# One-core ViT layer: v in fp32r for two images at a time, scores in 32x32 pieces, first-half probabilities in rows of 32

## The chip, the cores and the metric

The kernel runs on one core of one Trainium2 chip. The metric is device time in microseconds (us) of that core; the median of three runs is given. Engines are called PE (TensorE, with PEld for its weight loads), DVE (VectorE), ACT (ScalarE) and POOL (GpSimd). SBUF is the on-chip working memory, PSUM the memory that PE writes, in eight banks of 128 x 512 fp32.

## The reference

64 images give 49 patches each, with a class token 50 tokens of 256 values. Patches are RMS-normalised, quantised, and multiplied by a quantised weight. Then comes causal attention at three "scales", whose windows all reach beyond the 50 tokens, so that each is a plain causal attention over 50 tokens with weights of its own; each is followed by a projection and a layer norm, and the three are mixed by a last projection. A quantised gated feed-forward network ends the layer.

```
h   = embed(quantised patches)                               # (64, 50, 256)
x   = layer_norm(h)
for i in range(3):                                           # three scales
    q, k, v = x @ Wq[i].T, x @ Wk[i].T, x @ Wv[i].T          # 16 heads of 16
    s   = 4 * q k^T, masked above the diagonal
    e   = exp(s - max(s));  w = e / (sum(e) + 1e-6)
    o_i = layer_norm((w v) @ Wo[i].T)
h   = h + layer_norm(concat(o_i) @ Wout.T);  y = layer_norm(h);  out = h + ffn(y)
# feed-forward: fake-quantised silu(y Wg) * (y Wu), whose largest absolute value over
# everything sets the step of the quantisation before the down projection
```

## The kernel before

**Stages.** The first block does embedding and attention for eight groups of eight images (`GROUPS`, `GB`), and quantises the weights of the feed-forward network in between. The second block (from line 1484 on POOL, 1507 on DVE, 1598 on PE) does gate and up projections for all groups, finds the largest product, then does the down projection.

**Units.** A group has six *s* steps: three scales times two sets of four images (`QB = 4`). Each s step has two *units* u, e = 0 and e = 1: queries 0 to 24 against keys 0 to 24 (`WIDTH[0] = 25`), and queries 25 to 49 against all 50 keys (`WIDTH[1] = 50`). So the kernel has 48 s steps and 96 units. Four images' queries stand in PSUM rows 0, 32, 64 and 96.

**Steps of one s step.** On PE `k` and `q` (line 1265) are six fp32r matmuls of 400 columns each for every half of a scale's 256 rows: a value is cut into a high and a low fp32r part, and three products are added. `v` (lines 1281, 1285) is done in plain fp32, image by image: even heads into rows 0 to 49, odd heads into rows 64 to 113. POOL `spread` (line 875) multiplies k by a mask over head rows into `k_bd`, with four copies for each 64 rows, in two instructions per pair of images. PE `scores` (line 1299 for the mask, 1308 for the products) works in tiles of 64 rows by 32 columns, 16 products a unit; e picks one half of `ps_s`, so two units' scores can stand in PSUM at once, and the step waits for `scores_read` of the unit before the last. DVE `max` (1085) finds the maxima, `soft` (1089) subtracts them and so frees `ps_s`; ACT takes the exponential (780); DVE sums and inverts (1097, 1102); POOL multiplies (884). PE `turn_p` (1323) transposes the probabilities, eight transpositions into two banks for each unit, since a head has a row of 64 also where 25 keys are used; ACT copies them to `pT` (789), two copies a unit. PE `heads` (1334) multiplies by v, which ACT copied block-diagonally to `v_bd` in two copies (773). PE `project` (1350) follows.

**Order.** Each engine walks its own list, written out by hand in `AT` (tick numbers per kind of step, sorted by `engine_order`). Steps of several groups interleave. All PE results but the scores go round four PSUM banks (`ps_w`, `bank_plan`); a step waits until the bank's reader, four fills back, is through. Engines issue in order: a waiting instruction holds up all behind it.

## Time and profile before

| what | value |
|---|---|
| median of three runs | 819.95 us (814.86 to 820.36) |
| the profiled execution | 819.57 us, of which 817.7 us are the span from the first to the last instruction |
| mean granted TensorE clock | 0.959 of full speed |
| PE busy | 728.1 us, 89% of the span |
| DVE busy | 649.7 us, 79% |
| POOL busy | 544.5 us, 67% |
| ACT busy | 519.0 us, 63% |

Rough stages of the span: 0 to 56 us loading, embedding of the first images and preparation of weights; 56 to about 697 us attention; about 712 to 778 us gate and up projections; the rest is the down projection and the store. A busy share is an average over its stretch. An engine that is hardly ever idle sets the pace of a stage; what the others do costs time only where they make that one wait.

### The profile page before, as it was taken

The page shows a single profiled execution, that of the slowest core. Times are in us where ns is not written, and L with a number is a line of the kernel's source. Part 1 is how long each engine was busy: PE and PEld are TensorE (multiplying, and loading weights), DVE is VectorE, ACT ScalarE, POOL GpSimd, SP SyncE. Part 2 cuts the span into 40 slices and gives each one's busy share as a digit, 9 for nine tenths or more (in the row PEclk, how much of TensorE's full clock was granted, in tenths as well). Part 3 has the DMA queues.
Part 4 walks back from the last instruction along what each step waited for, and adds up shares of the span by engine and source line. Part 5 has one row for each costly group of instructions (what it writes and reads, how often), then busy time and mean ns, then how long its engine had stood idle before and what let it go on. Part 6 is the DMA issues. An engine that isn't in the chain of part 4 may idle for free. (4 is left out here: it accounts for less than half of the span.)

```text
span 817.7 us, 28887 instructions
## 1 busy us (share of the span) xinstructions
PE 728.1 (89%) x11302; PEld 573.7 (70%) x11302; DVE 649.7 (79%) x1346; ACT 519.0 (63%) x1085; POOL 544.5 (67%) x817
## 2 busy tenths in 40 slices
PE   1488999999999999999999999999999999377565
PEld 1265887788878787878777887878888787244354
DVE  4679676889788888888898789888987895758857
ACT  3546857646766576667556675675666665278684
POOL 2569757685786688858857866887768764421165
PEclk9869999999999999999999999999999999679979
DMA  8200000000000000000000000000101000000014
GB/s 243 88 15 31 14 20 17 18 17 18 18 17 17 18 16 18 18 18 31 3 18 18 16 18 18 18 31 3 38 3 38 20 3 20 0 1 0 0 32 129
DMA packets 14968, 22.09 MB, mean 27 GB/s; under 512 B 1972, under 2 KB 11446, under 8 KB 14840
## 3 DMA queue, kind: packets, MB, share of 16 engines
q1 hardware_dynamic: 14404, 19.91, 7.7%
q8 instruction: 90, 1.47, 0.7%
q10 hardware_dynamic: 436, 0.40, 0.2%
q14 instruction: 38, 0.31, 0.1%
HBM read 17.03 MB, written 3.28 MB: 25 GB/s over the span
## 5 line engine op out<-in xcount | busy, mean ns | idle before, releaser
L875 POOL TENSOR_TENSOR k_bd<-kT,rmask 128x400 f32<-128x400 f32 x192 | 167.4, 901 | 19.2 <-ACT kT L757 11.8
L884 POOL TENSOR_TENSOR prob<-prob,rsum 128x400 f32<-128x400 f32 x96 | 117.2, 1235 | 25.3 <-DVE rsum L1102 25.3
L789 ACT COPY pT<-ps_w 128x400 f32<-128x400 f32 x192 | 85.4, 507 | 29.1 <-PE ps_w L1323 28.3
L1285 PE MATMUL ps_w<-wv_sb,xf 128*50 128x128 f32 x1536 | 99.2, 272 | 0.0
L1323 PE MATMUL ps_w<-pack,prob 128*128 128x128 f32 x768 | 95.1, 275 | 1.8 <-DVE hidden L1062 0.9
L1350 PE MATMUL ps_w<-oy_hi,o_hi 128*128 128x512 f32 x192 | 93.6, 488 | 0.0
L1323 PEld LDWEIGHTS ps_w<-pack,prob 128*128 128x128 f32 x768 | 84.1, 141 | 11.9 <-issue 8.5
L1085 DVE TENSOR_REDUCE nmax<-ps_s 128x16 f32<-128x400 f32 x96 | 72.5, 770 | 9.7 <-PE ps_s L1308 9.2
L1097 DVE TENSOR_REDUCE rsum<-prob 128x16 f32<-128x416 f32 x96 | 74.1, 781 | 6.4 <-ACT prob L780 6.3
L803 ACT ACTIVATE ps_w<-ps_w 128x256 f32<-128x256 f32 x96 | 35.5, 370 | 68.8 <-PE ps_w L1350 68.4
L1285 PEld LDWEIGHTS ps_w<-wv_sb,xf 128*50 128x50 f32 x1536 | 78.1, 125 | 0.3
L780 ACT ACTIVATE prob<-prob 128x400 f32<-128x400 f32 x96 | 67.2, 714 | 15.9 <-DVE prob L1089 15.5
L1350 PE MATMUL ps_w<-oy_lo,o_hi 128*128 128x512 f32 x192 | 76.1, 396 | 0.0
L773 ACT COPY v_bd<-ps_w 50x512 f32<-50x512 f32 x96 | 55.8, 581 | 31.8 <-PE ps_w L1285 30.0
L1089 DVE TENSOR_TENSOR prob<-ps_s,nmax 128x400 f32<-128x400 f32 x96 | 72.7, 769 | 3.5 <-ACT pT L789 3.1
L1350 PE MATMUL ps_w<-oy_hi,o_lo 128*128 128x512 f32 x192 | 75.5, 393 | 0.0
L1308 PE MATMUL ps_s<-k_bd,qT 64*25 64x200 f32 (+1 forms) x3072 | 71.2, 293 | 0.0
L1265 PE MATMUL ps_w<-xh,qk_hi 128*128 128x400 f32 x192 | 70.2, 366 | 1.1 <-POOL xl L864 0.9
L1265 PE MATMUL ps_w<-xl,qk_hi 128*128 128x400 f32 x192 | 66.5, 346 | 0.0
L1265 PE MATMUL ps_w<-xh,qk_lo 128*128 128x400 f32 x192 | 66.4, 346 | 0.0
L889 POOL TENSOR_TENSOR ln<-ln,ln_eps 128x1 f32<-128x1 f32 x96 | 19.3, 201 | 69.0 <-ACT ps_w L803 68.6
L891 POOL TENSOR_TENSOR ln<-ln,neg_half 128x1 f32<-128x1 f32 x96 | 53.4, 557 | 7.5
(216 smaller groups left out, 1756.0 us busy)
## 6 DMA issues: line engine op xcount, KB each, us to landing
x_in<-in_x SPq DMA_DIRECT2D x64, 147.0 KB
out<-hidden SPq DMA_DIRECT2D x16, 200.0 KB
pT<-in_tok_w SPq DMA_DIRECT2D x1, 768.0 KB, 6.6
hidden<-in_wq SPq DMA_DIRECT2D x1, 768.0 KB, 8.4
k_bd<-in_wk SPq DMA_DIRECT2D x1, 768.0 KB, 9.2
wv_sb<-in_wv SPq DMA_DIRECT2D x1, 768.0 KB, 8.9
hidden<-in_wout SPq DMA_DIRECT2D x1, 768.0 KB, 8.9
hidden<-in_wo SPq DMA_DIRECT2D x1, 768.0 KB, 11.0
```

Source lines behind the costliest of these rows:

```text
L780: nc.scalar.activation(pr, pr, ACT.Exp).then_inc(exp_ready, 1)
L789: nc.scalar.copy(pT[:, s % 2, 4 * a:4 * a + 4, :, e * LQ:(e + 1) * LQ], ps_w[:, bank].rearrange("p (j t) -> p j t", j=4)[:, :, 0:QB * LQ]. ...
L875: last = nc.gpsimd.tensor_tensor(k_bd[:, v % KBD, c], kT[:, w % 2, c, 2 * p * L:(2 * p + 2) * L].unsqueeze(1).broadcast_to([P, HR, 2 * L]) ...
L884: nc.gpsimd.tensor_tensor(pr, pr, rsum[:, s % 2, e, 1].unsqueeze(2).broadcast_to([P, H, WIDTH[e]]), ALU.mult).then_inc(prob_ready, 1)
L1085: nc.vector.tensor_reduce(top, s_ps, AX.X, ALU.max, negate=True).then_inc(max_ready, 1)
L1089: nc.vector.tensor_tensor(prob[:, s % 2, e, :, 0:WIDTH[e]].rearrange("p (r h) t -> p r h t", r=2), s_ps, top.unsqueeze(3).broadcast_to([P, ...
L1097: nc.vector.tensor_reduce(rsum[:, s % 2, e, 0], prob[:, s % 2, e, :, 0:WIDTH[e] + 1], AX.X, ALU.add).then_inc(sum_ready, 1)
L1265: mm = nc.tensor.matmul(G[:, 0:GT], wt[:, w, q, k, c * P:(c + 1) * P], xt[:, k], start=(t == 0), stop=(t == 3 * KC - 1))
L1285: mm = nc.tensor.matmul(G[row:row + L, cols], xf[:, k, tokens], wv_sb[:, w, k, e], start=False, stop=(k == KC - 1), skip_group_check=True)
L1308: mm = nc.tensor.matmul(ps_s[32 * b:32 * b + LQ, e, r, c * HR * W:(c + 1) * HR * W], qT[rows, w % 2, c, first:first + LQ], k_bd[rows, v % ...
L1323: mm = nc.tensor.transpose(G[:, j * P:(j + 1) * P], flat[:, (4 * a + j) * P:(4 * a + j + 1) * P], pack[:])
L1350: mm = nc.tensor.matmul(G[:], ot[:, s % 2, c, 2 * (p % 2):2 * (p % 2) + 2].rearrange("p b t -> p (b t)"), wt[:, w, c], start=False, stop=( ...
```

## The change

- `v`: weights are cut into fp32r parts `wv_hi` and `wv_lo` (one ACT cast, one DVE subtraction), and two images are one stationary operand of 128 columns (`xh` and `xl` now give each image 64 columns). A step is two times one bias matmul and six fp32r matmuls of 256 columns. ACT takes v apart with four copies of 50 x 256 where it had two of 50 x 512.
- `spread`: two copies of k for each 32 rows, one instruction of 128 x 400 per pair of images where it had two.
- `scores`: tiles of 32 rows by 32 columns, 32 products a unit, each of half the columns. The four row groups write four banks, that is all of `ps_s`, for either e. So the step waits for `scores_read` of the last unit: one unit's scores at a time.
- `turn_p`, e = 0: probabilities have rows of 32 (`prob_lo`), so four transpositions into one bank do; ACT takes them apart with four copies of 25 partitions x 400. e = 1 is as before.
- Feed-forward: the maximum over a group's 2400 columns (line 1558) is taken in three pieces of 800, each placed after the next product.
- At the start: four small loads of the mask from ACT's queue, zeroing of `pT`, `v_bd` loaded with Wv first and zeroed once it is cut.
- All lists of `AT` are new. In the new PE list some other work stands between any two steps of scores; in the old one 39 of the 95 neighbours follow each other directly.

```diff
-    order = [... for a in range(2 if step[0] == "turn_p" else 1)]
+    order = [... for a in range(2 if step[0] == "turn_p" and step[1] % 2 else 1)]
...
@@ ACT
+                if kind == "wv_hi":
+                    act.wait_ge(loads["wv"], 16)
+                    nc.scalar.copy(wv_hi[:], by_row(st_v)).then_inc(split_v, 1)
...
                     for row, e in HALVES:
-                        nc.scalar.copy(v_bd[row:row + L, s % 2, :, :, e * HD:(e + 1) * HD],
-                                       ps_w[row:row + L, bank, :].rearrange("p (b j d) -> p b j d", b=QB, j=HP)).then_inc((v_even, v_odd)[e], 1)
+                        for src, b in HALVES:
+                            last = nc.scalar.copy(v_bd[row:row + L, s % 2, b::2, :, e * HD:(e + 1) * HD], v_ps[src:src + L, :, e])
+                    last.then_inc(v_ready, 1)
...
+                    if e == 0:
+                        bank, fill = bank_of(step)
+                        act.wait_ge(filled[bank], fill)
+                        act.wait_ge(zeroed, 4)
+                        for c in range(KC):
+                            for h in (0, 1):
+                                row = 32 * (2 * c + h)
+                                last = nc.scalar.copy(pT[ROWB * h:ROWB * h + LQ, s % 2, c::2, :, 0:LQ],
+                                                      ps_w[row:row + LQ, bank].rearrange(...)[:, :, 0:QB * LQ].rearrange(...))
+                        last.then_inc(pt_read, 1)
...
@@ POOL
                     if j == 0:
+                        pool.wait_ge(v_split, 1)
                         nc.gpsimd.memset(v_bd[:], 0.0).then_inc(zeroed, 1)
...
-                    for c in range(KC):
-                        last = nc.gpsimd.tensor_tensor(
-                            k_bd[:, v % KBD, c], kT[:, w % 2, c, 2 * p * L:(2 * p + 2) * L].unsqueeze(1).broadcast_to([P, HR, 2 * L]),
-                            rmask[:].unsqueeze(2).broadcast_to([P, HR, 2 * L]), ALU.mult)
-                    last.then_inc(kbd_ready, 1)
+                    nc.gpsimd.tensor_tensor(
+                        k_bd[:, v % KBD], kT[:, w % 2, :, 2 * p * L:(2 * p + 2) * L].unsqueeze(2).broadcast_to([P, KC, 2, 2 * L]),
+                        rmask[:].unsqueeze(1).unsqueeze(3).broadcast_to([P, KC, 2, 2 * L]), ALU.mult).then_inc(kbd_ready, 1)
...
@@ PE
-                    for b in range(QB):
-                        cols = slice(b * P, (b + 1) * P)
-                        tokens = slice((QB * q + b) * L, (QB * q + b + 1) * L)
-                        for row, e in HALVES:
-                            nc.tensor.matmul(G[row:row + L, cols], ones16[:, 0:L], bias3[:, (e * NS + w) * P:][:, 0:P],
-                                             start=True, stop=False, skip_group_check=True)
+                    for a in (0, 1):
+                        cols = G[:, a * D:(a + 1) * D]
+                        two = slice(QB * q + 2 * a, QB * q + 2 * a + 2)
+                        nc.tensor.matmul(cols, ones16[:], v_bias[:, w], start=True, stop=False)
                         for k in range(KC):
-                            for row, e in HALVES:
-                                mm = nc.tensor.matmul(G[row:row + L, cols], xf[:, k, tokens], wv_sb[:, w, k, e],
-                                                      start=False, stop=(k == KC - 1), skip_group_check=True)
+                            for xt, wt in ((xh, wv_hi), (xh, wv_lo), (xl, wv_hi)):
+                                mm = nc.tensor.matmul(cols, xt[:, k, two].rearrange("p b t -> p (b t)"), wt[:, w, k], start=False,
+                                                      stop=(k == KC - 1 and xt is xl))
...
-                    pe.wait_ge(scores_read, U * m + u - 1 + AHEAD)
+                    pe.wait_ge(scores_read, U * m + u + AHEAD)
...
                     for c in range(KC):
-                        for r in (0, 1):
-                            rows = slice(r * ROWB, (r + 1) * ROWB)
-                            for b in range(QB):
-                                first = (QB * q + b) * L + e * LQ
-                                v = 2 * s + b // 2
-                                mm = nc.tensor.matmul(ps_s[32 * b:32 * b + LQ, e, r, c * HR * W:(c + 1) * HR * W],
+                        for b in range(QB):
+                            first = (QB * q + b) * L + e * LQ
+                            v = 2 * s + b // 2
+                            for r in range(4):
+                                rows = slice(32 * r, 32 * r + 32)
+                                mm = nc.tensor.matmul(row_ps[32 * b:32 * b + LQ, r, c * 2 * W:(c + 1) * 2 * W],
                                                       qT[rows, w % 2, c, first:first + LQ],
                                                       k_bd[rows, v % KBD, c, :, (b % 2) * L:(b % 2) * L + W],
                                                       start=False, stop=True, skip_group_check=True)
...
-                    for a in (0, 1):
+                    for a in range(1 + e):
                         G = ps_w[:, bank_of(step, a)[0]]
...
@@ DVE, feed-forward
+            def largest(g, j, done):
+                dve.wait_ge(acts_ready, done + T)
+                nc.vector.tensor_reduce(hmx[:, bass.ds(g * FC + 2 * j, 2)], acts[:, 2 * j:2 * j + 2, bass.ds(g * GT, GT)], AX.X, ALU.max,
+                                        apply_absolute_value=True).then_inc(acts_max, 1)
...
+                    if j > 0:
+                        largest(g, j - 1, n)
+                largest(g, FP - 1, g * FP + FP)
```

## Rows read from the trace of the kernel before

**Rows 1.** The page's first part: busy us, share of the span, instructions.
```profile
PE 728.1 (89%) x11302; PEld 573.7 (70%) x11302; DVE 649.7 (79%) x1346; ACT 519.0 (63%) x1085; POOL 544.5 (67%) x817
```

**Rows 2.** Busy time by stretch: stretch, its length, busy us per engine, clock, DMA.
```profile
60.00:80.00 20.00, 15.92 (x300) 12.33 (x299) 19.55 (x22) 12.49 (x20) 19.38 (x17) 0.96 0.10 32
140.00:540.00 400.00, 396.14 (x6713) 321.50 (x6712) 337.51 (x752) 261.28 (x577) 300.61 (x482) 1.00 0.06 18
740.00:760.00 20.00, 14.20 (x96) 7.88 (x96) 17.94 (x17) 17.37 (x31) 3.13 (x3) 1.00 0.00 0
```

**Rows 3.** Waits of PE, 140 to 540 us, the longest: us, times, longest.
```profile
PE ps_s L1299 <- DVE prob L1089: 1.4, 2, 1.2
```

**Rows 4.** Waits of DVE, 140 to 540 us: first and last of 16.
```profile
DVE nmax L1085 <- PE ps_s L1308: 8.2, 9, 3.0
...
DVE acc L1132 <- DVE ln L1130: 0.2, 1, 0.2
```

**Rows 5.** Timeline of PE, 400 to 430 us: start, duration, merged instructions.
```profile
400.49 0.39 PE L1350 MATMUL ps_w<-oy_hi,o_hi 128*128 128x512 f32 x1
400.72 0.40 PE L1350 MATMUL ps_w<-oy_lo,o_hi 128*128 128x512 f32 x1
...
401.28 0.26 PE L1299 MATMUL ps_s<-mask,pick 64*128 64x200 bf16 x2
401.47 0.57 PE L1308 MATMUL ps_s<-k_bd,qT 64*25 64x100 f32 x32
401.97 0.34 PE L1299 MATMUL ps_s<-mask,pick 64*128 64x400 bf16 x2
402.24 0.90 PE L1308 MATMUL ps_s<-k_bd,qT 64*25 64x200 f32 x32
403.08 0.83 PE L1247 MATMUL ps_w<-tokT,x_qT 128*128 128x256 bf16 x6
...
409.35 0.24 PE L1281 MATMUL ps_w<-bias,ones 96*50 96x128 bf16 x2
...
411.36 0.22 PE L1281 MATMUL ps_w<-bias,ones 96*50 96x128 bf16 x2
...
415.44 1.97 PE L1323 MATMUL ps_w<-pack,prob 128*128 128x128 f32 x16
417.25 0.50 PE L1238 MATMUL ps_w<-id,x_q 128*128 128x128 bf16 x6
...
419.81 1.83 PE L1334 MATMUL ps_w<-pT,v_bd 128*32 128x50 f32 x128
421.57 0.24 PE L1281 MATMUL ps_w<-bias,ones 96*50 96x128 bf16 x2
```

**Rows 6.** Groups of instructions by form: busy us, mean ns, idle before.
```profile
L875 POOL TENSOR_TENSOR k_bd<-kT,rmask 128x400 f32<-128x400 f32 x192 | 167.4, 901 | 19.2 <-ACT kT L757 11.8 <-PE ps_s L1308 7.2
L789 ACT COPY pT<-ps_w 128x400 f32<-128x400 f32 x192 | 85.4, 507 | 29.1 <-PE ps_w L1323 28.3
L773 ACT COPY v_bd<-ps_w 50x512 f32<-50x512 f32 x96 | 55.8, 581 | 31.8 <-PE ps_w L1285 30.0
L1085 DVE TENSOR_REDUCE nmax<-ps_s 128x16 f32<-128x800 f32 x48 | 47.0, 980 | 2.4 <-PE ps_s L1308 2.1
L1089 DVE TENSOR_TENSOR prob<-ps_s,nmax 128x800 f32<-128x800 f32 x48 | 46.8, 975 | 0.5 <-ACT pT L789 0.3
L1265 PEld LDWEIGHTS ps_w<-xl,qk_hi 128*128 128x128 f32 x192 | 36.5, 190 | 0.6
L1247 PE MATMUL ps_w<-tokT,x_qT 128*128 128x256 bf16 x192 | 29.0, 292 | 2.5 <-ACT x_qT L737 2.0 <-issue 0.4
L1558 DVE TENSOR_REDUCE hmx<-acts x6 | 15.9, 2653 | 0.9
```

**Rows 7.** PE's timeline cut to 401.465 to 401.472, and to 401.40 to 401.53.
```profile
401.47 0.26 PE L1308 MATMUL ps_s<-k_bd,qT 64*25 64x100 f32 x1
...
401.47 0.31 PE L1308 MATMUL ps_s<-k_bd,qT 64*25 64x100 f32 x8
```

356 lines of the change are left out of this document (193 added, 163 removed), and 131 rows, old and new, of the table AT.

## The prediction

> **What bounds the kernel now.** I read four views, from coarse to fine. The page's first part [rows 1] shows PE busiest, but as a mean over unlike stages. The table by stretch [rows 2] says where: over 400 us in the middle of attention PE is busy 396, DVE 338, POOL 301 and ACT 261, at full clock. The list of PE's waits there [rows 3] has hardly anything: its longest entry is 1.4 us in all. So in attention the time is the sum of PE's steps, and a microsecond taken out of them is a microsecond of the kernel as long as nobody else becomes late. Who would? DVE's waits in the same stretch are 16 entries, first and last in [rows 4], which add up to 47 us. So 400 - 47 = 353 us are taken, by work of 338 and small gaps of 15: DVE is at 88%, nearer to PE than its busy share says. The stretch from 60 to 80 us is another case: POOL and DVE are full and PE is idle for 4 of 20 us. In gate and up projections (740 to 760) DVE is full with 17.9 of 20.
>
> From PE's timeline [rows 5] I take each step from its start to the start of the next. v takes 411.36 - 409.35 = 2.01 us. Scores take 0.69 for e = 0 (401.28 to 401.97) and 1.11 for e = 1 (to 403.08), of which the mask is 0.19 and 0.27. Two transposing steps take 1.81, or 0.91 each. Two steps of heads, 128 matmuls, take 1.76.
>
> **v.** The nearest fp32r matmul, line 1350, has 512 columns and comes every 400.72 - 400.49 = 0.23 us [rows 5], 0.45 ns a column; for 256 columns 0.115. The bias matmul of 256 bf16 columns is like line 1247, six in 0.83 where one lasts 0.29 [rows 5, 6]: (0.83 - 0.29) / 5 = 0.11 from start to start. A half is 0.11 + 6 x 0.115 = 0.80, a step 1.60, and I add 0.05 for the first load: 1.65. Gain 0.36 x 48 = 17 us. The other bound is a load that can't hide behind so short a matmul: the load row of line 1265 says 190 ns [rows 6], which makes 2 x (0.11 + 6 x 0.19) = 2.5 us and a loss of 24. I take the first: the fp32 transpositions load 128 columns as well and come every 0.11 us [rows 5], so a load's record is longer than what it holds up.
>
> **Transpositions, e = 0.** Four for eight: 0.45 of 0.91, times 48, is 22 us. Nothing is unknown here.
>
> **Scores.** 32 products a unit, two matmul instructions each: 64 for 32. Their columns are halved and the tiles doubled, so each tile has half the work, for twice the instructions in all, and what counts is how fast they start. The cut of the timeline [rows 7] shows one lasting 0.26 and eight together 0.31, so eight start within 0.05 us, some 7 ns apart. At the other end are the heads, 1.76 / 128 = 13.8 ns [rows 5], where four tiles share the work, so that the array itself may be what limits. After the last start today's e = 0 takes 0.50 - (0.57 - 0.25) = 0.18 until the next step (with 0.25 for the last matmul). I take 7 ns, the burst's: 0.19 + 0.45 + 0.18 = 0.82 for either e. The pair is 1.64 for 1.80, gain 0.16 x 48 = 8 us. At 13.8 ns it is 2.5, a loss of 34.
>
> The Trainium skill speaks against this part. "TensorE: Matmul & The Clock Gate", section "Back-to-back issue gap", gives about 25 ns as the least distance of two matmuls however few the columns. By it a unit would take 64 x 0.025 + 0.37 = 1.97 us and the change would lose 103 us here. The trace doesn't agree for products in different tiles: 32 of them begin within 0.32 us.
>
> Sum on PE: 17 + 22 + 8 = 47 us of some 640 us of attention. k, q, heads and projections keep their matmuls and columns; the padded rows of `xh` change a stride only.
>
> **The other engines.** POOL: 96 instructions of 0.9 us fall away (line 875, [rows 6]), 86 us in all, and nothing is added but some zeroing at the start; in the stretch it goes from 301 of 400 us to about 247 of 370, or 67%. This helps the ramp at 60 to 80 us. It may help DVE too. The Trainium skill, "SBUF — State Buffer", section "Who interferes with whom", says that VectorE and GpSimd lock one pair of ports against each other; by it DVE gains a few microseconds here, which no row here prices and the sum leaves out.
>
> ACT: for e = 0 four copies of 400 columns for two, at 0.51, are 1.0 us more for each of 48 steps [rows 6]: 49 us. v: four of 256 columns; from 400 columns at 0.507 and 512 at 0.581 a column is 0.66 ns, so 0.41 each, 1.65 for 1.16, or 24 us. Together 73 us over attention: from 65% of 641, 419 us, to 492 of 594, or 83%. It has no price while its copies come in time; they free PE's banks, four fills back.
>
> DVE: same work in attention, in a stage that is 7% shorter: 353 of 370, 95%. This is the cover that gets thin.
>
> **The new wait.** One unit's scores at a time: the step of unit u + 1 waits for `soft` of u, and behind it on PE stands everything else, since PE issues in order; ACT, POOL and DVE then wait for PE. After a unit's scores DVE needs 0.98 for the maxima and 0.975 for the subtraction (e = 1; [rows 6]), with hand-overs about 2.2 us; e = 0 about 1.3. I added up the new PE list with the times above: of 95 distances between scores, 9 hold less than 2 us of other PE work and 22 less than 2.5. A DVE that is a little late (it has other steps between) makes PE wait there. I put this, with DVE and ACT nearly full, at 0.15 us a unit: 14 us. Net in attention 47 - 14 = 33.
>
> **Feed-forward.** A group's maximum in three pieces: 800 columns are 2.65 / 3 = 0.88 at least and 0.98 by line 1085 [rows 6], so 0 to 0.3 us more on the full engine in each of eight groups; against it a piece fills the gap before a group's last product, and the last group's end has two pieces behind the last product for one of 2.65. I take 1 us gain, plus or minus 2.
>
> **Start.** wv is cut (ACT about 1.5 us, DVE about 2.3), `v_bd` is zeroed only then, and POOL's next steps stand behind that wait; against it are the faster spreads. I take 0, plus or minus 4.
>
> Working against the profiled execution, 819.6 us (817.7 of span), whose difference to the median of 819.95 is nothing: 819.6 - 33 - 1 = 786 us.
>
> **The rivals.**
> - *All of it arrives.* The order fits, nobody is late, and the ramp gives 4: 819.6 - 47 - 1 - 4 = 768. For it: PE's waits are near nothing now. Against: DVE at 95%. Chance 0.15.
> - *Half is eaten.* DVE or ACT is late more often and PE waits 0.35 us a unit, 34 us: 819.6 - 47 + 34 - 1 = 806. For it: the two shares. Chance 0.18.
> - *A bound of a matmul is wrong.* Loads of 190 ns make v a loss: 786 + 41 = 827; or products start at the heads' pace: 786 + 42 = 828. Against: the transpositions, the burst. Chance 0.10 for both.
> - *Slower by the single buffer.* Place: the mask matmul at the head of scores. PE waits for `soft` unit by unit; it decides at 47 / 96 = 0.5 us a unit, and with 0.75 it is 819.6 - 47 + 72 = 845. Against: other work is placed between all scores, where 39 of 95 were neighbours. Chance 0.08.
> **How the numbers follow.** The forecast, 786 with 776 to 799 of its own, has 0.48. For faster by over 1% (below 811; about what a measurement here can tell) I add 0.48, 0.15 and most of the half-eaten case: 0.78. Within 1% get the rest of it and most of the wrong bounds: 0.12. Slower: 0.10. The range of 8 in 10 goes from the full gain to just past the half-eaten case, 765 to 815; beyond lie the slow cases with their 0.2.
>
> **What would show it.** v from start to next start: 1.6 to 1.7 (2.5: loads don't hide). Scores: about 0.8 for either e, 64 starts 7 ns apart (14: the other bound). Transpositions of e = 0: 0.45. PE's waits at the mask line for DVE `prob`: some 14 us in attention; 50 or more and the single buffer has won. DVE's waits shrink from 47 of 400 to some 20 of 370. POOL's spread is 96 x 0.9. If ACT stands at 83% and PE waits at `turn_p` or `heads` for ACT's `pT`, the four copies are the reason. I am wrong if PE's steps shrink by 47 us and the time doesn't follow, or if they don't shrink.

## The result and the profile after

The changed kernel takes 806.48 us (median of 4 runs, 804.51 to 808.14) where the kernel before, beside it, takes 819.55 (814.86 to 820.36): ratio 0.9851, with a 95% interval of 0.9808 to 0.9895. The profiled execution took 806.6 us with a span of 804.8, against a span of 817.7 before. That is 13 us faster, where 34 were forecast; 806 is the number of the rival in which half of the gain is eaten; whether its mechanism is the one that acted is taken up at the end.

First the page of the changed kernel and its table by stretch, with the columns of [rows 1] and [rows 2]:

```profile
PE 710.1 (88%) x13126; PEld 567.1 (70%) x13126; DVE 639.9 (80%) x1363; ACT 584.2 (73%) x1278; POOL 462.3 (57%) x728
```

```profile
60.00:80.00 20.00, 17.95 (x353) 13.75 (x351) 16.25 (x27) 15.38 (x25) 15.16 (x19) 1.00 0.11 33
140.00:540.00 400.00, 386.00 (x7931) 318.17 (x7931) 338.59 (x760) 301.19 (x694) 248.25 (x416) 1.00 0.06 19
740.00:760.00 20.00, 17.24 (x112) 9.18 (x110) 20.00 (x25) 17.50 (x31) 3.24 (x3) 1.00 0.00 0
```

In the 400 us in the middle of attention PE has lost 10 us of its fullness, ACT has gained 40, POOL has lost 52 and DVE stands where it was, since the stage did not get shorter. That is the second reading. I cut both traces at the start of the first k or q product, of the last product of attention's projections and of the last maximum of the feed-forward part:

| part, us | before | after | difference |
|---|---|---|---|
| up to the first k or q product | 55.8 | 52.3 | -3.5 |
| attention, to its last projection | 643.1 | 643.9 | +0.8 |
| from there to the last maximum (gate and up) | 76.3 | 68.1 | -8.2 |
| the rest | 42.6 | 40.5 | -2.1 |

So the stage at which the change was aimed gave nothing, and the 13 us come from around it (the rest holds the last maximum itself, which is a piece of 0.9 us where it was 2.6). Within attention I add up PE's time by step (each matmul from its start to the next one's start, idle time apart):

| PE in attention, us | before | after | forecast difference | measured |
|---|---|---|---|---|
| v | 99.7 | 82.7 | -17 | -17.0 |
| transposed probabilities | 87.7 | 71.0 | -22 | -16.7 |
| scores | 87.7 | 95.8 | -8 | +8.1 |
| k and q | 112.0 | 118.8 | 0 | +6.8 |
| projections | 158.0 | 159.4 | 0 | +1.4 |
| all other steps | 87.0 | 92.3 | 0 | +5.3 |
| PE idle | 10.8 | 23.7 | +14 | +12.9 |

Of the 5.3 in "other steps", 3.4 are two short steps (`bo_fold`, `y_spread`) that stood before the first k product and now stand behind it; that is the 3.5 us of the start, so the start gained nothing by itself.

A part of the growth is the granted clock, which the prediction took as full. In the changed kernel 15.4 us of attention lie at half clock: the first 5.1, which are the end of a stretch that began before attention, and three stretches of 3.4, each begun 0.4 to 2 us after PE had stood still for 1.9, 1.4 and 1.4 us. In the kernel before it is one stretch of 6.8 us. The three stretches, with the columns of [rows 2], and k and q products in the second one:

```profile
453.40:456.80 3.40, 3.40 (x79) 2.92 (x79) 0.68 (x1) 2.82 (x6) 2.79 (x3) 0.50 0.34 100
600.10:603.50 3.40, 3.39 (x11) 2.99 (x12) 3.02 (x5) 2.71 (x7) 1.62 (x3) 0.51 0.03 5
692.30:695.70 3.40, 3.40 (x9) 2.36 (x8) 2.99 (x11) 0.48 (x2) 1.92 (x5) 0.50 0.01 2
```

```profile
601.91 0.54 PE L1307 MATMUL ps_w<-xh,qk_lo 128*128 128x400 f32 x1
602.24 0.54 PE L1307 MATMUL ps_w<-xh,qk_hi 128*128 128x400 f32 x1
```

These products come every 0.33 us where they come every 0.19 at full clock. By such distances my estimate is that half clock makes up 2 of the 6.8 us of k and q, 1.8 us of the transpositions and all of the 1.4 of the projections, some 5 us of PE's steps in all.

The timeline of PE after, with start, duration and merged instructions, as in [rows 5]:

```profile
403.90 0.22 PE L1340 MATMUL ps_s<-mask,pick 32*128 32x100 bf16 x4
404.05 0.80 PE L1349 MATMUL ps_s<-k_bd,qT 32*25 32x50 f32 x64
404.78 0.45 PE L1307 MATMUL ps_w<-xh,qk_hi 128*128 128x400 f32 x1
405.07 0.35 PE L1307 MATMUL ps_w<-xl,qk_hi 128*128 128x400 f32 x1
...
405.82 0.35 PE L1307 MATMUL ps_w<-xh,qk_lo 128*128 128x400 f32 x1
406.02 0.28 PE L1323 MATMUL ps_w<-bias,ones 96*128 96x256 bf16 x1
...
406.26 0.28 PE L1326 MATMUL ps_w<-wv_lo,xh 128*128 128x256 f32 x1
406.38 0.28 PE L1326 MATMUL ps_w<-wv_hi,xl 128*128 128x256 f32 x1
...
407.70 1.03 PE L1364 MATMUL ps_w<-pack,prob_hi 128*128 128x128 f32 x8
...
409.32 0.27 PE L1340 MATMUL ps_s<-mask,pick 32*128 32x200 bf16 x4
409.52 0.96 PE L1349 MATMUL ps_s<-k_bd,qT 32*25 32x100 f32 x64
410.41 0.51 PE L1280 MATMUL ps_w<-id,x_q 128*128 128x128 bf16 x6
...
418.65 0.66 PE L1364 MATMUL ps_w<-pack,prob_lo 128*128 128x128 f32 x4
419.14 0.27 PE L1323 MATMUL ps_w<-bias,ones 96*128 96x256 bf16 x1
```

v takes 407.70 - 406.02 = 1.68 us and its matmuls come every 0.12; the four transpositions take 419.14 - 418.65 = 0.49; the scores take 0.88 (403.90 to 404.78) and 1.09 (409.32 to 410.41), together 1.97 for 1.80 before. The k and q matmuls come every (405.82 - 405.07) / 4 = 0.187 us.

PE's waits and DVE's in the same 400 us, with the columns of [rows 3] and [rows 4], the longest of each:

```profile
PE ps_w L1297 <- ACT v_bd L793: 2.1, 2, 1.1
PE ps_s L1340 <- DVE prob_lo L1131: 2.0, 3, 1.3
PE ps_w L1280 <- issue: 1.9, 1, 1.9
PE ps_w L1385 <- DVE o_lo L1151: 1.5, 1, 1.5
```

```profile
DVE nmax L1127 <- PE ps_s L1349: 11.8, 13, 3.9
DVE acc L1162 <- issue: 7.7, 11, 2.8
```

There are 13 kinds of waits of PE, 13.0 us in all, where there were 6 with 3.7 us. None is over 2.1 us: they are small ones, for ACT and for DVE, all over the stage. No single one has taken the place of the work removed. DVE's waits add up to 45 us where they were 47; the prediction's sign was some 20 of 370. The costliest groups of ACT and POOL, with the columns of [rows 6]:

```profile
L813 ACT COPY pT<-ps_w 25x400 f32<-25x400 f32 x192 | 94.7, 493 | 7.7 <-PE ps_w L1364 5.1
L793 ACT COPY v_bd<-ps_w 50x256 f32<-50x256 f32 x192 | 70.5, 367 | 18.8 <-PE ps_w L1326 16.3
```

```profile
L915 POOL TENSOR_TENSOR k_bd<-kT,rmask 128x400 f32<-128x400 f32 x96 | 83.5, 885 | 36.6 <-ACT kT L775 21.9 <-PE ps_s L1349 14.7
```

Over attention the durations of ACT's instructions, added up, went from 474 to 539 us (+65), POOL's from 495 to 414 (-81), DVE's from 585 to 581. Neighbours overlap a little, so the busy times are smaller: ACT 420 to 489, POOL 477 to 403, DVE 531 to 529.

### The profile page after: what moved, and what is told of

Read it like the earlier page. It is cut to its first block and busy times, and to the rows that moved or that the text cites. A ratio compares the mean times of both kernels' runs of the same rounds, so it can differ in the third digit from the quotient of the medians.

```text
span 804.8 us, 32634 instructions
## 1 busy us (share of the span) xinstructions
PE 710.1 (88%) x13126; PEld 567.1 (70%) x13126; DVE 639.9 (80%) x1363; ACT 584.2 (73%) x1278; POOL 462.3 (57%) x728
## 5 line engine op out<-in xcount | busy, mean ns | idle before, releaser
L915 POOL TENSOR_TENSOR k_bd<-kT,rmask 128x400 f32<-128x400 f32 x96 | 83.5, 885 | 36.6 <-ACT kT L775 21.9
L813 ACT COPY pT<-ps_w 25x400 f32<-25x400 f32 x192 | 94.7, 493 | 7.7 <-PE ps_w L1364 5.1
L923 POOL TENSOR_TENSOR prob_hi<-prob_hi,rsum 128x800 f32<-128x800 f32 x48 | 75.1, 1565 | 37.0 <-DVE rsum L1144 37.0
L1127 DVE TENSOR_REDUCE nmax<-ps_s 128x16 f32<-128x400 f32 x96 | 74.1, 772 | 23.8 <-PE ps_s L1349 23.1
L1349 PE MATMUL ps_s<-k_bd,qT 32*25 32x50 f32 (+1 forms) x6144 | 84.9, 231 | 0.4 <-issue 0.4
L793 ACT COPY v_bd<-ps_w 50x256 f32<-50x256 f32 x192 | 70.5, 367 | 18.8 <-PE ps_w L1326 16.3
L1349 PEld LDWEIGHTS ps_s<-k_bd,qT 32*25 32x25 f32 x6144 | 61.6, 97 | 13.2 <-issue 0.7
L1326 PE MATMUL ps_w<-wv_hi,xh 128*128 128x256 f32 x192 | 62.1, 323 | 0.0
L923 POOL TENSOR_TENSOR prob_lo<-prob_lo,rsum 128x400 f32<-128x400 f32 x48 | 42.6, 888 | 28.6 <-DVE rsum L1144 28.5
L1326 PE MATMUL ps_w<-wv_lo,xh 128*128 128x256 f32 x192 | 54.1, 282 | 0.0
L1326 PE MATMUL ps_w<-wv_hi,xl 128*128 128x256 f32 x192 | 54.0, 281 | 0.0
L1364 PE MATMUL ps_w<-pack,prob_hi 128*128 128x128 f32 x384 | 52.3, 279 | 0.5 <-ACT v_bd L793 0.3
```

Source lines behind the costliest of these rows:

```text
L793: last = nc.scalar.copy(v_bd[row:row + L, s % 2, b::2, :, e * HD:(e + 1) * HD], v_ps[src:src + L, :, e])
L813: last = nc.scalar.copy(pT[ROWB * h:ROWB * h + LQ, s % 2, c::2, :, 0:LQ], ps_w[row:row + LQ, bank].rearrange("p (j t) -> p j t", j=4)[:, : ...
L915: nc.gpsimd.tensor_tensor(k_bd[:, v % KBD], kT[:, w % 2, :, 2 * p * L:(2 * p + 2) * L].unsqueeze(2).broadcast_to([P, KC, 2, 2 * L]), rmask ...
L923: nc.gpsimd.tensor_tensor(pr, pr, rsum[:, s % 2, e, 1].unsqueeze(2).broadcast_to([P, H, WIDTH[e]]), ALU.mult).then_inc(prob_ready, 1)
L1127: nc.vector.tensor_reduce(top, s_ps, AX.X, ALU.max, negate=True).then_inc(max_ready, 1)
L1326: mm = nc.tensor.matmul(cols, xt[:, k, two].rearrange("p b t -> p (b t)"), wt[:, w, k], start=False, stop=(k == KC - 1 and xt is xl))
```

## The experiments

Differences "by the ratio" are against the kernel before or the changed kernel, as 819 us times the difference of the ratios; the interval of a ratio is 2 to 6 thousandths to either side, so 2 to 5 us. A difference between two runs has both intervals in it: against the changed kernel, whose own is 4 thousandths, it is good to 4 to 6 us. Where an edit's diff is shown cut, "..." stands for what is left out. Attention's length and PE's steps are those of one profiled execution, and how long it stood at half clock differs too (in us of attention: before 6.8, changed 15.4).

### The feed-forward part by itself

The kernel before, with only the maximum in three pieces:

```diff
-                nc.vector.tensor_reduce(hmx[:, bass.ds(g * FC, FC)], acts[:, :, cols], AX.X, ALU.max, ...
...
+                    if j > 0:
+                        largest(g, j - 1, n)
+                largest(g, FP - 1, g * FP + FP)
```

> The kernel before, with only the maximum of the feed-forward network taken in three pieces. Theory 1 (read from the two traces): the gain of the whole change sits behind attention, where the period of a group of gate and up fell from 6.45 to 5.69 us; this piece alone gives it, 819.6 - 10 = about 810 us, and a period of 5.7. Rival (the prediction's own step): the pieces give 1 us, plus or minus 2, and the period falls because of something else, so about 819 and a period of 6.3 to 6.5.

Measured: 813.1 us, ratio 0.9915 (0.988 to 0.9949), so 7 us. Attention 644.1; to the last maximum 71.5 (-4.8), the rest 40.5 (-2.1). DVE's timeline in gate and up projections, first before, then with this edit:

```profile
743.53 2.65 DVE L1558 TENSOR_REDUCE hmx<-acts  x1
746.10 0.98 DVE L1553 TENSOR_TENSOR acts<-ps_s,gate 128x800 f32 x1
...
748.85 0.99 DVE L1553 TENSOR_TENSOR acts<-ps_s,gate 128x800 f32 x1 [0.55 <-ACT gate L1449]
749.98 2.65 DVE L1558 TENSOR_REDUCE hmx<-acts  x1
```

```profile
741.83 0.98 DVE L1558 TENSOR_TENSOR acts<-ps_s,gate 128x800 f32 x1
742.73 1.86 DVE L1548 TENSOR_REDUCE hmx<-acts  x2
744.52 0.98 DVE L1558 TENSOR_TENSOR acts<-ps_s,gate 128x800 f32 x1
...
746.63 0.97 DVE L1548 TENSOR_REDUCE hmx<-acts  x1
747.53 0.98 DVE L1558 TENSOR_TENSOR acts<-ps_s,gate 128x800 f32 x1
```

A group goes from 749.98 - 743.53 = 6.45 us to 747.53 - 741.83 = 5.70. The pieces hardly lengthen the work (three times 0.9 from start to start for 746.10 - 743.53 = 2.57), and they fill the gaps in which DVE stood between products: together 0.75 us a group, and two pieces less behind the last product. So 7 of the 13 us are this edit. The prediction's own 1 us, the rival here, is out. Another 3.4 come from the handover, which only the changed kernel has (last projection to last maximum: 68.1 against 71.5). The traces put them on DVE: its last instruction of attention ends 8.8 us after the last projection starts (705.0 - 696.2), with this edit alone 12.2 us (712.1 - 699.9). The new order leaves it less to do at the end; which entry of the list does it was not tried.

### ScalarE: two of the four copies left out

```diff
-                        for c in range(KC):
+                        for c in range(1):
                             for h in (0, 1):
                                 ... last = nc.scalar.copy(pT[ROWB * h:..., s % 2, c::2, :, 0:LQ], ...)
```

> The changed kernel, with two of the four copies of the first-half probabilities left out (the half of the heads keeps zeros there, so the output is another): 96 instructions and 47 us less on ACT. Theory 2 (ACT at 75 to 80% of attention holds PE's banks too long): 8 us or more faster, 798 or less. Theories 1 and 3: within 2 us of 806.5.

Measured: 795.97 us, ratio 0.9715 (0.9671 to 0.9759), 11 us less than the changed kernel. Attention 632.4, 11.5 less, of which PE's idle time is 5.7 (23.7 to 18.0) and 5.8 lie inside the steps. Of these some 4 are the clock: 6.6 us of attention are at half clock, where it was 15.4. ACT's work has a price although ACT is busy for only 75% of the stretch.

### Padded rows in the kernel before

`xh` and `xl` with rows of 64 for images of 50 tokens, as the change has them, in the kernel before. To have the space, the low part of the output weights is replaced by the high part.

```diff
-    xh = sb(att, "xh", [P, KC, GT], F32R)
+    xh = sb(att, "xh", [P, KC, GB, ROWB], F32R)
...
-  nc.tensor.matmul(G[:, 0:GT], wt[:, w, q, k, c * P:(c + 1) * P], xt[:, k], ...
+  nc.tensor.matmul(G[:, 0:GT], wt[:, w, q, k, c * P:(c + 1) * P], xt[:, k, :, 0:L], ...
```

> The kernel before, with the rows of xh and xl padded from 50 to 64 columns for each image; for want of SBUF the low part of the output projection's weights is not kept (that matmul reads the high part again, so the output is less exact; every instruction stays). Theory 1: the padded rows make the 400-column matmuls of k and q slower, 0.19 us from start to start for 0.18, and the kernel 6 to 8 us slower, 826 to 828. Rival: k and q are longer in the changed kernel through hidden waits, and padding costs nothing: 820, plus or minus 1.5, and 0.18 us.

Measured: 818.48 us, ratio 0.9987 (0.9963 to 1.0012). Its timeline, with the x columns read in runs of 50 out of 64:

```profile
404.82 0.35 PE L1265 MATMUL ps_w<-xl,qk_hi 128*128 128x400 f32 x1
...
406.74 0.35 PE L1265 MATMUL ps_w<-xh,qk_lo 128*128 128x400 f32 x1
```

Ten matmuls on, 1.92 us: 0.192 each, against 0.182 in the kernel before. The k and q steps take 115.4 us for 112.0, PE's idle time falls from 10.8 to 7.8, and the time is unchanged. Theory 1 was right on the 0.19 and wrong on the time, its rival the other way round. So "the padded rows of `xh` change a stride only" was wrong for the steps, and no harm to the time could be measured. That is only a weak sign that PE's time doesn't count one for one, since this execution had no half clock in attention where the kernel before has 6.8 us of it. Without that the padding costs k and q some 4.4 us, and with the 2 us of half clock this makes up nearly all of their 6.8.

### The first half in rows of 64 again

The changed kernel, with eight transpositions and two copies for e = 0 as before:

```diff
-    prob_lo = sb(att, "prob_lo", [P, 2, H, 32])
+    prob_lo = sb(att, "prob_lo", [P, 2, H, ROWB])
...
-                    for a in range(1 + e):
+                    for a in (0, 1):
```

> The changed kernel, with the first-half probabilities in rows of 64 again: eight transpositions and two copies a unit. PE has some 20 us more to do and ACT 49 us less. Theory 2 (ACT is the late one): both cancel, 806 plus or minus 6. Theory 3 (only PE's own work counts): 806 + 20 = 826.

Measured: 833.05 us, ratio 1.0183 (1.0132 to 1.0233), 27 us slower than the changed kernel. Attention 668.3 (+24.4): steps +19.3, idle +5.1, although ACT has 46 us less. Here PE's work counted in full, and ACT's relief did not show. The time is 7 us beyond even theory 3's 826. Each of these steps also fills two banks of the ring where the change fills one; whether that is the surplus was not tried.

### Score products of 64 rows again, with two buffers and with one

The changed kernel with the scores in tiles of 64 rows by 32 columns, `k_bd` with four copies again, made by 192 instructions of POOL. To have the space, the low part of the output weights is replaced by the high part in the projections. The two runs differ in one line, the wait of the step:

```diff
-                        nc.gpsimd.tensor_tensor(k_bd[:, v % KBD], ...[P, KC, 2, 2 * L]..., ALU.mult)
+                        for c in range(KC):
+                            last = nc.gpsimd.tensor_tensor(k_bd[:, v % KBD, c], ...[P, HR, 2 * L]..., ALU.mult)
...
-                    pe.wait_ge(scores_read, U * m + u + AHEAD)
+                    pe.wait_ge(scores_read, U * m + u - 1 + AHEAD)    # two buffers only
```

> The changed kernel with its new order, but scores in tiles of 64 rows by 32 columns as before, two buffers, and POOL's spread in two instructions (86 us more on POOL); for want of SBUF the low part of the output projection's weights is replaced by the high part. Scores take 0.17 us less a pair, 8 us in all. Theory 1 (the single buffer costs waits): those 8 and another 8 or more, 790 or less. Rival (the single buffer costs nothing in this order): 806.5 - 8 = 798, plus or minus 3. If POOL's larger load matters: 803 or more.

> The same as the run with 64x32 scores and two buffers, but the step waits for the subtraction of the last unit as in the changed kernel: the pair differs in nothing but the single buffer. Theory 1: 8 us or more slower than its partner. Rival: within 2 us of it.

Measured: with two buffers 818.71 us, ratio 1.0013 (0.9982 to 1.0044), attention 656.4; with one 827.83, ratio 1.0108 (1.0071 to 1.0145), attention 666.5. The stretch from 140 to 540 us with two:

```profile
140.00:540.00 400.00, 373.10 (x5775) 293.67 (x5774) 333.15 (x742) 295.28 (x683) 292.22 (x471) 1.00 0.06 17
```

and one product step of either half in its timeline:

```profile
404.01 0.57 PE L1351 MATMUL ps_s<-k_bd,qT 64*25 64x100 f32 x32
...
408.30 0.90 PE L1351 MATMUL ps_s<-k_bd,qT 64*25 64x200 f32 x32
```

Two things follow. The single buffer costs 8 to 10 us here, so it is a real price, far from that of the rival that ends slower (72). And the 64-row products are the shorter ones on PE (scores 88.5 us for 95.8), yet with them and two buffers the kernel is 12 to 14 us slower, and PE's idle time is 43.2 for 23.7. POOL has 85 us more (292 of 400 for 248), and PE's list of waits in the 400 us now names POOL's products of the probabilities (5.5 us of 26.5), which the changed kernel's doesn't; its two longest entries are for DVE (4.5 and 4.2). So the case of load on POOL, 803 or more, is the one that holds, and both theories on the buffer (790 or less, 798) are out for the run with two. What the small products bring is POOL's relief, not PE's time. The pair prices the single buffer for 64-row products. For the 32-row products, which fill all four banks in one unit, no run has a second buffer.

### v in plain fp32 again

```diff
-    xh = sb(att, "xh", [P, KC, GB, ROWB], F32R)
+    xh = sb(att, "xh", [P, KC, GB, L], F32R)
...
-                            for xt, wt in ((xh, wv_hi), (xh, wv_lo), (xl, wv_hi)):
-                                mm = nc.tensor.matmul(cols, xt[:, k, two]..., wt[:, w, k], ...
+                            for row, e in HALVES:
+                                mm = nc.tensor.matmul(G[row:row + L, cols], xf[:, k, QB * q + b], wv_sb[:, w, k, e], ...
```

> The changed kernel with one part undone: v again in plain fp32 over unpadded `xh` and `xl`, 2 copies of v_bd a unit pair of halves instead of 4; scores, maxima and rows of 32 stay as changed. On TensorE v's step goes back from 1.7 to 2.0 us (+17 us over 48 steps) and the k and q steps lose the 3.4 to 6.8 us that the padded rows cost; ScalarE gets some 24 us back. Theory A (TensorE's own time counts nearly in full, ScalarE's lateness with the slope of the run without two copies, 10.5 us for 47): 806.5 + 17 - 5 - 5 = 813, from 810 to 817. Rival B (what TensorE is given there only becomes a wait, since the vector engines set the time): attention within 2 us of the changed kernel's 643.9, or shorter by ScalarE's 5 us, and the time 801 to 808.

Measured: 817.31 us, ratio 0.9988 (0.9959 to 1.0017), 11 us slower than the changed kernel; attention 651.9 (+8.0), steps +9.9 (v +18.7, k and q -7.1), idle -2.0. Theory A's 810 to 817 is just missed, B's 801 to 808 is out. In the changed kernel's order, work added to PE counts nearly in full, although ACT has 15 us less here.

### Work moved off ScalarE, and taken off it

The first edit moves 32 instructions from ACT to POOL, the second leaves them on ACT and does them on 64 of 768 columns.

```diff
-                    nc.scalar.activation(x_t[:], x_in[:, p % 2], ACT.Identity, scale=xs[:, 6, p:p + 1], bias=magic[:])
+                    nc.gpsimd.tensor_scalar(x_t[:], x_in[:, p % 2], xs[:, 6, p:p + 1], MAGIC, ALU.mult, ALU.add)
```

> The changed kernel with 32 instructions of 1.03 us (the rounding shift of x in the group stages) moved from ScalarE to GpSimd, at the same place of the order; everything is computed. ScalarE is relieved of 33 us, GpSimd, at 62% in the stretch from 140 to 540 us, gets some 33 to 50. Theory A (ScalarE is late): by the slope of 10.5 us for 47, the time falls by 7 us to 799 or 800, with TensorE's idle time in attention falling from 23.7 to about 20. Rival B (GpSimd's load slows VectorE and comes late itself, as in the run with 64-column scores and two buffers): no gain or a loss, 806 to 812, and VectorE's instructions of x_q longer than 697 ns.

```diff
-                    nc.scalar.activation(x_t[:], x_in[:, p % 2], ACT.Identity, ...
+                    nc.scalar.activation(x_t[:, 0:64], x_in[:, p % 2, 0:64], ACT.Identity, ...
```

> The changed kernel with the rounding shift of x in the group stages done on 64 of 768 columns (the output is another): ScalarE has 32 instructions of some 0.3 us for 1.03 us, 23 us less over attention, and no other engine gets or loses work. In the run that moved these instructions to GpSimd nothing was gained; here GpSimd isn't loaded for it. Theory A (ScalarE's load as a whole makes it late): with the slope of the run without two copies (10.5 us for 47 us) the time falls by 5 us, to 801 or 802, TensorE's idle time in attention from 23.7 to some 20. Theory B (what costs is the latency of the four copies between the transpositions and what waits for their bank and for `pT`, not ScalarE's load): less than 2 us, 804 to 807.

Measured: moved, 808.2 us, ratio 0.9896 (0.9863 to 0.9928), attention 643.0 and idle 25.3: no gain, perhaps a loss. Taken off, 801.17 us, ratio 0.9754 (0.9732 to 0.9776), 8 us less than the changed kernel by the ratio and 5 by the median, attention 636.7, idle 20.6. In attention the durations of ACT's instructions add up to 28 us less in the first and 17 less in the second. Of the 7.2 us of attention some 4 lie inside PE's steps and go with the clock (6.6 us at half clock for 15.4). So it is ACT's load as such, not only the copies' place, that costs, and 28 us more on POOL, in a stretch where it was busy for 62%, seem to cost about what 28 us less on ACT give.

### VectorE: half of the sum, half of the maximum

```diff
-  nc.vector.tensor_reduce(rsum[...], prob[e][:, s % 2, :, 0:WIDTH[e] + 1], AX.X, ALU.add)
+  nc.vector.tensor_reduce(rsum[...], prob[e][:, s % 2, :, 0:WIDTH[e] // 2 + 1], AX.X, ALU.add)
```

> The changed kernel with one edit that changes the result: the sum of the probabilities is taken over half of the columns, which takes about 35 us from VectorE in attention and nothing from any other engine. Theory A (VectorE is late, too): the time falls by 8 us or more, to 798 or less. Rival B (VectorE isn't what TensorE waits for; ScalarE and the single buffer of scores are): less than 2 us, 804 to 807.

```diff
-  nc.vector.tensor_reduce(top, s_ps, AX.X, ALU.max, negate=True)
+  nc.vector.tensor_reduce(top, s_ps[:, :, :, 0:WIDTH[e] // 2], AX.X, ALU.max, negate=True)
```

> The changed kernel with the maximum taken over half of the columns of each head's scores (the output is another): VectorE has 37 us less in attention, about as much as the 35 us less of the run with half the sum, which gave 3 us. But this work lies between a unit's last product and the release of the only score buffer, so the buffer is held 0.4 us (first half 0.2, second 0.5) less per unit, 96 times. Theory A (TensorE's waits and steps at the single buffer are what costs): clearly more than 3 us, 8 to 15, so 792 to 799, and TensorE's idle time in attention from 23.7 to 15 or less. Theory B (the buffer isn't what costs in this order; only VectorE's load): 3 us like the half sum, 802 to 805.

Measured: the sum, 803.73 us, ratio 0.9827 (0.9768 to 0.9885), attention 640.9 (-3.0), idle 21.9; the maximum, 801.83 us, ratio 0.9756 (0.9732 to 0.9779), attention 639.3 (-4.6), idle 23.2. Both take 30 us from DVE. The engine that looked fullest after PE gives back least: 2 to 3 us, which is within the noise. The same work between the last product and the release of `ps_s` gives 5 to 8, which is theory A's sign, but the idle time that it named (15 or less) did not come. That the two edits differ is not shown: their intervals meet, and the 1.6 us between their attentions are less than the clock can make, since the run with half the sum has 15.0 us of attention at half clock and the run with half the maximum 7.0. With the pair above, the buffer has a price of some us, and its size in this order stays open.

### Copies split between two engines

Two of the four copies on DVE, with a semaphore of their own:

```diff
-                        for c in range(KC):
+                        for c in (0,):
...
+                if kind == "turn_lo":
+                    for h in (0, 1):
+                        row = 64 + 32 * h
+                        last = nc.vector.tensor_copy(pT[ROWB * h:ROWB * h + LQ, s % 2, 1::2, :, 0:LQ], ps_w[row:row + LQ, bank]...)
```

> The changed kernel, everything computed, with two of the four copies of the first half's transposed probabilities moved from ScalarE to VectorE: ScalarE has 47 us less, VectorE 48 x 2 x 0.5 = 48 us more (from 85% in the stretch from 140 to 540 us to about 96%), and the four copies lie on two engines side by side, 1 us from the transpositions to the last copy for 2. Theory A (latency of the copies): most of the 10.5 us of the run that left two copies out, less what VectorE's load costs by the half-sum run's slope (3 us for 35, so 4): 799 to 801. Theory B (VectorE, nearly full, comes late for the single score buffer): no gain or a loss, 806 to 820, with VectorE's waits in attention gone and TensorE's idle time above 24.

Measured: 849.65 us, ratio 1.0331 (1.0302 to 1.0361). DVE's group of these copies and PE's two longest waits in the 400 us:

```profile
L1147 DVE COPY pT<-ps_w 25x400 f32<-25x400 f32 x96 | 55.1, 574 | 10.4 <-PE ps_w L1381 8.6
```

```profile
PE ps_s L1357 <- DVE prob_lo L1135: 4.8, 5, 2.2
PE ps_w L1324 <- DVE pT L1147: 3.6, 2, 2.1
```

That is beyond both theories. Attention is 692.3 us, 48 longer: 35 of it are PE's idle time (59), 13 lie in PE's steps. 36 us of attention are at half clock, so most of the 13 go with the clock and not with work: PE's pauses seem to be paid for twice. DVE is busy for 583 of the 692 us, 84%, where it was 82% with 54 us less work. So the stage grew by nearly as much as DVE's work, and the 16% in which it stands idle were not room for it. It can be relieved without much gain and not loaded.

### The same questions in the order of the kernel before

The runs so far stand in the changed kernel's order. Three runs in the old order take the two sides of the sum apart: v over one of two parts of its contraction (PE 42 us less), ACT's copies for e = 0 cut into rows 0 to 63 and 64 to 127 (ACT 49 us more), and both.

```diff
-                        for k in range(KC):
-                            for row, e in HALVES:
-                                mm = nc.tensor.matmul(G[row:row + L, cols], xf[:, k, tokens], wv_sb[:, w, k, e], ...
+                        for row, e in HALVES:
+                            mm = nc.tensor.matmul(G[row:row + L, cols], xf[:, 0, tokens], wv_sb[:, w, 0, e], ...
```

> The kernel before with v's product over one of the two 128-row parts of its contraction (the output is another): four of each eight fp32 matmuls fall away, 0.22 us four times a step, 48 steps: 42 us less on TensorE, about what the prediction expected of v and the transpositions together (39), and nothing changes on another engine. Theory A (TensorE's sum sets attention, microsecond for microsecond, as the prediction read the waits): 819.5 - 42 = 777, from 775 to 781. Theory B (ScalarE, VectorE and GpSimd are so near that a part becomes waits): 25 us or less, so 794 or more, with TensorE's idle time in attention growing from 10.8 to 25 or more.

```diff
-                        nc.scalar.copy(pT[:, s % 2, ...], ps_w[:, bank]...).then_inc(pt_read, 1)
+                        for rows in (slice(0, 64), slice(64, P)) if e == 0 else (slice(0, P),):
+                            last = nc.scalar.copy(pT[rows, s % 2, ...], ps_w[rows, bank]...)
+                        last.then_inc(pt_read, 1)
```

> The kernel before with ScalarE's two copies of the first half's transposed probabilities each cut into two of 64 rows: four copies of 0.5 us for two, 96 x 0.5 = 49 us more on ScalarE in attention, the same data, TensorE, VectorE and GpSimd unchanged. Theory A (ScalarE's load and the latency of these copies are paid in part, 0.24 us per us as in the changed kernel): 10 to 15 us slower, 829 to 835. Theory B (the prediction's reading: no price while the copies come in time, since ScalarE goes from 65% to 73% only): less than 2 us, 818 to 822.

> Both edits at once in the order of the kernel before: TensorE 42 us less, ScalarE 49 us more (the output is another). Theory A (the added copies are what eats the gain): the time lies 15 us or more above the run with TensorE's work alone, since the stage is shorter and ScalarE fuller: 792 to 802 if that one is at 777. Theory B (they don't): within 4 us of that run. Theory C (the parts add up): the sum of the two single effects within 3 us.

Measured:

| | us | ratio to before | attention | PE's steps | PE idle |
|---|---|---|---|---|---|
| before | | 1 | 643.1 | 632.1 | 10.8 |
| PE 42 less | 806.2 | 0.9807 (0.9758 to 0.9857) | 628.8 | 597.2 | 31.3 |
| ACT 49 more | 844.93 | 1.0288 (1.0228 to 1.0348) | 665.3 | 642.1 | 23.1 |
| both | 828.19 | 1.0086 (1.0052 to 1.012) | 643.0 | 603.3 | 39.5 |

The stretch from 140 to 540 us of the three, in this order:

```profile
140.00:540.00 400.00, 383.64 (x6430) 302.90 (x6414) 345.22 (x770) 266.05 (x588) 306.69 (x490) 1.00 0.06 18
```

```profile
140.00:540.00 400.00, 389.83 (x6590) 311.43 (x6589) 327.96 (x731) 284.50 (x613) 289.16 (x462) 1.00 0.06 18
```

```profile
140.00:540.00 400.00, 377.10 (x6165) 294.84 (x6167) 337.00 (x750) 289.90 (x632) 298.07 (x478) 1.00 0.06 17
```

and PE's longest waits in the first:

```profile
PE ps_w L1322 <- DVE acc L1120: 3.6, 6, 1.9
PE ps_s L1298 <- DVE prob L1089: 3.0, 1, 3.0
PE ps_w L1284 <- issue: 1.7, 2, 0.9
```

Theory B holds in the first: v's steps lost 40.2 us, attention 14.3, and 20.5 came back as idle time, with no engine but PE over 87%. Taking a microsecond from PE was worth 0.35 to 0.4. The second is beyond even theory A: 49 us on an engine busy for 65% cost 22 to 24 us, nearly half of each. PE's list of waits has six entries for ACT's `pT` (L790), none over 1.2 us; the kernel before has none for it. 10 of the 22 us are not in its idle time but inside its steps, though PE's work is the same and only 3.4 us are at half clock: 7.4 of them in the transpositions, whose banks these copies free. A transposition's record lasts 0.28 us where the starts are 0.11 apart, so a short wait of the next one doesn't show as idle time. By the ratios the two effects add up (-16 and +24 make +8, measured +7, theory C). The attention lengths (+7.9 by addition, -0.1 measured) don't contradict it: the profiled execution of both edits took 821.45 us, 6.7 less than the median of its ten. So removing 42 us of PE and adding 49 of ACT is no gain but a loss of some 7 us. The changed kernel's own trade is of this kind, -34 us in v and the transpositions for +65 of ACT; it has POOL's relief on top.

## Why the prediction was right and wrong

**What bounds the kernel.** This step failed first: "in attention the time is the sum of PE's steps, and a microsecond taken out of them is a microsecond of the kernel as long as nobody else becomes late". The sum was right as bookkeeping (632.1 of 643.1) and wrong as a slope. That PE hardly waits [rows 3] shows that every release comes just in time, not that it comes early. With 42 us less on PE, the releases of DVE, POOL and ACT were late by half of that (idle time +20.5). The condition, "as long as nobody else becomes late", was read from shares (88, 75 and 65% in the stretch), and a share says nothing of the distance between a release and the step that needs it. Nor is the slope the same both ways: work put back on PE in the changed order (plain v, the first half's transpositions) cost about its full length. Whether that is the direction or the order was not separated, since no run takes work from PE alone in the changed order or adds it to PE alone in the old one.

**v.** Right: 1.68 us for 1.65, and 17.0 us of the stage. Fp32r matmuls of 256 columns come every 0.12 us, so their weight loads hold nothing up.

**Transpositions.** The step is right (0.49 for 0.45). The stage gives 16.7 of 22. A part of the missing 5.3 is 0.04 x 48 = 2; another 1.8 are stretches at half clock, which fell on three of these steps. In six of the runs in the changed order these steps take 69.0 to 70.0 us for 71.0, whichever engine was relieved. The last 1.5 us are open.

**Scores.** The term with the wrong sign: +8.1 for -8. From the rows above, 64 products take 0.80 and 0.96 with the last one's duration in it; with 0.21 to 0.25 for that, the starts are 9 ns apart for e = 0 and 11 for e = 1. The burst of eight [rows 7] gave 7 and did not last over 64. The error is 0.33 us a pair, 16 us in all. e = 1 is slower than e = 0 with the same count, so at twice the columns the number of starts is no longer all that counts; the prediction had both at 0.82. The 14 ns of the heads and the 25 ns of the last rival did not come.

**Unchanged steps.** "The padded rows of `xh` change a stride only" failed: k and q took 6.8 us more. Some 4.4 are the padding (3.4 as measured alone, plus 1 us of half clock that the kernel before has and that run hasn't), 2 are half clock.

**The new wait.** 14 us were put down for it and PE's idle time grew by 12.9; the rows show that it is only in part the wait named, for `soft` at the mask line (2.0 us of 400). Most are waits for ACT's and DVE's results at other steps. So the number came out right by luck: the buffer's mechanism was given all of it and had a small part. The single buffer cost 8 to 10 us where it was tried. And the waits cost more than themselves, by the half clock that followed them, which no term of the sum had.

**ScalarE.** "It has no price while its copies come in time" is the costliest sentence. The growth was sized well (65 us for 73), the price was 0.45 to 0.5 us for each added in the order of the kernel before and 0.24 to 0.42 for each taken away in the changed one (11.5 for 47, 7.2 for 17, the clock included): so, as an estimate, 15 to 32 us, up to nearly all that v and the transpositions gave (34). The text before the prediction had the means of it: four banks go round, and most of their fills wait for a copy of ACT's or a result of DVE's.

**GpSimd.** 81 us for 86 and 96 instructions of 0.885, as forecast, but with no price beyond "This helps the ramp". In the ramp, between 60 and 80 us, POOL is busy for 15.16 us where it had 19.38 [rows 2], and PE for 17.95 where it had 15.92. But it is in all of attention that it carries the scores' edit, by 12 to 14 us. The prediction also said, of DVE and POOL in each other's way, that it "may help DVE too" (the Trainium skill, "SBUF — State Buffer", section "Who interferes with whom"). The traces agree, in one group of DVE's, the instruction that makes `x_q`. In the kernel before, one of these stands beside a product of POOL's:

```profile
493.26 1.86 DVE L1049 TENSOR_SCALAR x_q<-x_t 128x768 bf16<-128x768 f32 x1 [0.20 <-ACT x_t L721]
```

```profile
493.17 1.53 POOL L884 TENSOR_TENSOR prob<-prob,rsum 128x800 f32<-128x800 f32 x1
```

Its shortest is 0.54 us; here it ends 0.4 us after POOL's instruction does. The whole group, before and after (minimum, median and maximum in ns):

```profile
L1049 DVE TENSOR_SCALAR x_q<-x_t x36: 542/688/5416, 16.8 to 677.1; 128x768 bf16<-128x768 f32 x36
```

```profile
L1088 DVE TENSOR_SCALAR x_q<-x_t x36: 497/560/2665, 20.3 to 678.1; 128x768 bf16<-128x768 f32 x36
```

By their means (991 and 697 ns) the 36 lose 10.6 us, which is more than the few microseconds of the prediction and about all that DVE's busy time fell over the whole span (649.7 to 639.9). With POOL's 85 us back (the 64-row products with two buffers) the mean is 791 ns: 3.4 of the 10.6 us return. The rest must lie in the new order, which sets what stands beside it, and was not separated. DVE's largest groups kept their durations (0.98 us for the maxima and the subtraction over 800 columns). What these 10.6 us brought in time, no run tells.

**VectorE.** Its work stayed (581 us for 585). At 85% of the stretch, not 95, it was not the cover that got thin in the sense of the prediction: 30 us less of it brought 2 to 3. But 54 us more of it cost 48, so it has no room either.

**Feed-forward and start.** -7 for -1 plus or minus 2. The mechanism was right and its size was not: the pieces cost 0.1 us a group, where 0 to 0.3 was feared, and what a group gains net is 0.75 us, eight times. The start was inside its bounds.

**The account.** By the steps that carried the sum: 47 us expected of PE became 12.1, of which 16 is the scores' term, 7 the k and q steps, 5 the transpositions, 7 the rest. The new waits came as sized, though not where they were put. Both together give +0.8 for -33 in attention. The 10 us behind attention, where 1 was forecast, make up a part of it, 3.5 more are two steps that changed sides. The rival "half is eaten" had the number, and that is luck: it put 34 us on waits and 1 us on the feed-forward part, and the runs show 13 and 10, with PE's own steps 35 us short. It had the kind of the waits (ACT or DVE late more often), but not the cause of the larger part, which is on PE itself.

**What stays open.** The price of POOL's load by itself in the order of the kernel before, the single buffer's for 32-row products, how much of all this is the hand-written order, and 1.9 us of other steps.

## What to carry to other kernels

Where four engines pass one ring of buffers round and the first has no waits, don't price its time at one for one and the others' at nothing. One run that takes work from the first engine and one that adds work to another, with the order unchanged, give both slopes (here 0.4 and 0.5); a change that trades one for the other then has an estimate before it is written. Measure each slope in the direction in which the change will move, and read the granted clock beside each stage's length: a few microseconds of "longer steps" were half clock here. A start distance read from a burst of eight is a lower bound for a step of 64, not its price.

## What the runs showed of the hardware

- Products in tiles of 32 rows and 32 columns, over 50 and 100 columns, start every 9 and 11 ns in a step of 64. The 32 products of the same unit in tiles of 64 rows, over 100 and 200 columns, take less time in all: 0.57 and 0.90 us for 0.80 and 0.96, the last one's duration included.
- An fp32r matmul of 400 columns takes 0.182 us from start to start with its columns in one run, and 0.187 to 0.192 with them in runs of 50 out of 64. At a granted clock of 0.5 the latter take 0.33.
- In the changed kernel's attention three pauses of PE of 1.4 to 1.9 us were each followed, 0.4 to 2 us after their end, by 3.4 us at half clock; with 59 us of pauses (the copies split between two engines) 36 us of attention were at half clock.
- A maximum over 800 columns takes 0.90 us from start to start and one over 2,400 takes 2.57 (2.65 in duration), so cutting it in three costs 0.1 us.
- An instruction of VectorE from SBUF to SBUF (768 columns, fp32 to bf16), 0.54 us at its shortest, took 1.86 us beside an instruction of GpSimd of 1.53.
- Cutting a copy of 128 partitions into two of 64 costs the whole duration again: 0.5 us each.
